# A recurrent step's input gate seeded into PSUM, and its two half sums added by one reduction

## What is computed

```
xw = einsum('ntd,dh->nth', x, Wx) + b
def step(h_prev, xw_t):
    h_next = tanh(xw_t + h_prev @ Wh)
    return h_next, h_next
x = x + scan(step, h0, xw)
```

## Time and profile before

| | |
|---|---|
| median of three runs | 1470.11 us |
| the profiled execution, its own time | 1471.73 us |
| its span | 1469.9 us |
| mean granted TensorE clock | 0.985 |
| TensorE busy | 1432.0 us (97%) |
| VectorE busy | 994.8 us (68%) |
| ScalarE busy | 659.7 us (45%) |
| first addition of step 0 starts | 32.02 us |
| products of the last step start | 1204.97 us |

### The profile page before, as it was taken

How to read it: one execution, slowest core, us unless ns; L and a number is a source line. 1 busy time by engine, 2 the same in 40 slices (tenths; PEclk the granted TensorE clock), 3 DMA queues, 4 the chain that set the end, 5 groups by cost and what they waited for, 6 DMA issues and landing times. The chain is left out here.

```text
span 1469.9 us, 49910 instructions
## 1 busy us (share of the span) xinstructions
PE 1432.0 (97%) x21212; PEld 1130.0 (77%) x21212; DVE 994.8 (68%) x2704; ACT 659.7 (45%) x2200; POOL 689.6 (47%) x555
## 2 busy tenths in 40 slices
PE   8889999999999999999999999999999998899998
PEld 6558888888888888888888888888887777577776
DVE  5334757575757575757575757575757679998894
ACT  4445454545454545454545454545444444233332
POOL 3432444444444444444444444444433446788774
PEclk8899999999999999999999999999999999999999
DMA  9750333333333323333323333333224547989994
GB/s 374 282 194 6 52 67 53 67 52 67 53 66 52 67 52 67 52 67 53 67 52 67 53 67 52 67 53 66 45 45 87 142 104 124 277 316 334 342 328 147
DMA packets 442337, 168.16 MB, mean 114 GB/s; under 512 B 406481, under 2 KB 409681, under 8 KB 438914
## 3 DMA queue, kind: packets, MB, share of 16 engines
q1 hardware_dynamic: 441584, 164.53, 44.4%
q10 hardware_dynamic: 530, 0.44, 0.1%
HBM read 96.78 MB, written 68.16 MB: 112 GB/s over the span
## 5 line engine op out<-in xcount | busy, mean ns | idle before, releaser
L462 PEld LDWEIGHTS recb<-hs,scanS 128*128 128x128 f16 x16384 | 443.7, 96 | 170.9 <-DVE hs L1265 169.6
L462 PE MATMUL recb<-hs,scanS 128*128 128x32 f16 x16384 | 495.0, 177 | 18.0 <-DVE hs L1265 17.9
L697 ACT ACTIVATE hs<-pre 128x64 f16<-128x64 f32 x512 | 131.7, 257 | 623.1 <-DVE pre L1257 622.3
L1255 DVE TENSOR_TENSOR pre<-recb,xw 128x64 f32<-128x64 f32 x512 | 115.1, 225 | 265.3 <-PE recb L462 261.4
L1120 DVE RECIPROCAL gates<-gates 128x64 f32<-128x64 f32 (+1 forms) x484 | 258.4, 555 | 0.4
L1265 DVE TENSOR_TENSOR hs<-konst,hs 128x64 f16<-128x64 f32 x512 | 115.1, 225 | 136.6 <-ACT konst L698 136.6
L949 POOL TENSOR_TENSOR xt<-xt,hbuf 128x512 f32<-128x512 f32 (+1 forms) x65 | 99.0, 1523 | 175.4 <-ACT hbuf L701 175.4
L937 POOL TENSOR_TENSOR x1lo<-xt,x1hi 128x512 fp32r<-128x512 f32 x64 | 82.1, 1284 | 186.8 <-ACT x1hi L707 186.8
L955 POOL TENSOR_TENSOR gates<-gates 128x512 f32<-128x512 f32 x62 | 80.0, 1290 | 166.6 <-DVE gates L1120 166.6
L962 POOL TENSOR_TENSOR xt<-xt,pout 128x512 f32<-128x512 f32 x64 | 75.8, 1185 | 153.6 <-DVE pout L1146 153.6
L1257 DVE TENSOR_TENSOR pre<-recb,pre 128x64 f32<-128x64 f32 x512 | 114.9, 224 | 17.6
(11 more groups left out here) (221 smaller groups left out, 2760.5 us busy)
## 6 DMA issues: line engine op xcount, KB each, us to landing
xt<-in_x SPq DMA_DIRECT2D x64, 256.0 KB, 3.6
g_d<-gst SPq DMA_DIRECT2D x64, 256.0 KB, 3.9
n_d<-nst SPq DMA_DIRECT2D x64, 256.0 KB, 3.1
x_d<-xt SPq DMA_DIRECT2D x64, 256.0 KB, 3.1
out<-gates SPq DMA_DIRECT2D x63, 256.0 KB, 6.6
xt<-x_d SPq DMA_DIRECT2D x28, 512.0 KB, 5.1
stage<-in_w SPq DMA_DIRECT2D x11, 1024.0 KB, 7.3
xt<-g_d SPq DMA_DIRECT2D x14, 512.0 KB, 7.4
```

What stands on the lines that cost most here:

```text
L462: last = nc.tensor.matmul(rec[:, m].rearrange("p a b -> p (a b)"), w[:, k, m * P:(m + 1) * P], hs[:, k].rearrange("p a b -> p (a b)"), sta ...
L697: nc.scalar.activation(hs[:, :, 0, :], pre[t % 2][:], ACT.Tanh, scale=unscale).then_inc(s_h, 1)
L1255: nc.vector.tensor_tensor(pre0[:], rec[:, :, 0, :], xw[j % 2][:, t], ALU.add).then_inc(s_pre0, 1)
```

## The change

The bank `recb` is split into two halves of 128 columns, one for even and one for odd steps (`sums`). Behind the operation that reads one half, VectorE writes the seed of the next step into the other half: the x gate in the columns of the high part and zero in those of the low part, made by one multiplication of the gate with the two numbers 1 and 0 (`halves`, in PSUM). The products of a step then all accumulate. One reduction over both parts gives `pre`. Since only TensorE's own writes mark PSUM elements as ones to accumulate onto, one extra product over the 256 columns stands ahead of the loop; and the first step's products wait for the first seed.

```diff
@@ tiles
-        pre0, pre = sb("pre0", [P, C, B]), [sb(f"pre{e + 1}", [P, C, B]) for e in range(2)]
+        pre = [sb(f"pre{e + 1}", [P, C, B]) for e in range(2)]
...
-        rec = recb[:, 0:C * 2 * B].rearrange("p (c a b) -> p c a b", c=C, a=2)
+        sums = [recb[:, e * SUMS:(e + 1) * SUMS].rearrange("p (c a b) -> p c a b", c=C, a=2) for e in range(2)]
+        halves = recb[:, 2 * P:2 * P + 2]
@@ SyncE, before the early loads of the last block
-                    sp.wait_ge(s_pre0, TS * (NBLK - 1))
+                    sp.wait_ge(s_pre, TS * (NBLK - 1))
@@ TensorE, step
-                            last = nc.tensor.matmul(rec[:, m].rearrange("p a b -> p (a b)"), w[:, k, m * P:(m + 1) * P],
-                                                    hs[:, k].rearrange("p a b -> p (a b)"),
-                                                    start=(k == 0 and m == 0 and w is wh_hi), stop=(k == C - 1),
-                                                    skip_group_check=True)
+                            last = nc.tensor.matmul(sums[t % 2][:, m].rearrange("p a b -> p (a b)"), w[:, k, m * P:(m + 1) * P],
+                                                    hs[:, k].rearrange("p a b -> p (a b)"), start=False, stop=(k == C - 1), skip_group_check=True)
@@ TensorE, before the loop
+            pe.wait_ge(s_turned, 3)
+            nc.tensor.matmul(recb[:, 0:2 * SUMS], split["x"][0][:, 0, 0:P], x1hi[:, 0, 0:2 * SUMS], start=True, stop=True).then_inc(s_bits, 1)
             pe.wait_ge(s_sg, 3)
             pe.wait_ge(s_wh, 9)
-            pe.wait_ge(s_turned, 3)
+            pe.wait_ge(s_seed, 1)
@@ VectorE
+            def seed(j, t):
+                j, t = j + t // TS, t % TS
+                if j == NBLK:
+                    return
+                if t == 0 and j:
+                    dve.wait_ge(s_xw, C * (j + 1))
+                gate = xw[j % 2][:, t].unsqueeze(2).to_broadcast([P, C, 2, B])
+                keep = halves.unsqueeze(1).unsqueeze(3).to_broadcast([P, C, 2, B])
+                nc.vector.tensor_tensor(sums[t % 2], gate, keep, ALU.mult).then_inc(s_seed, 1)
...
-            dve.wait_ge(s_h0, 1)
+            dve.wait_ge(s_bits, 1)
+            nc.vector.memset(halves[:, 0:1], 1.0)
+            nc.vector.memset(halves[:, 1:2], 0.0).then_inc(s_h0, 1)
+            dve.wait_ge(s_h0, 2)
+            seed(0, 0)
             for j in range(NBLK):
                 for t in range(TS):
-                    if t == 0:
-                        dve.wait_ge(s_xw, C * (j + 1))
                     dve.wait_ge(s_rec, TS * j + t + 1)
-                    nc.vector.tensor_tensor(pre0[:], rec[:, :, 0, :], xw[j % 2][:, t], ALU.add).then_inc(s_pre0, 1)
-                    dve.wait_ge(s_pre0, TS * j + t + 1)
-                    nc.vector.tensor_tensor(pre[t % 2][:], rec[:, :, 1, :], pre0[:], ALU.add).then_inc(s_pre, 1)
+                    nc.vector.tensor_reduce(pre[t % 2][:], sums[t % 2].rearrange("p c a b -> p c b a"), axis=AX.X, op=ALU.add).then_inc(s_pre, 1)
+                    seed(j, t + 1)
```

More of the change, by code:

```diff
@@ L84 @@
 SLOTS = B * C
+SUMS = C * 2 * B
 def build(nc, a, out):
@@ L194, in build @@
                                     "s_hyp s_lr s_h0").split())
-        (s_x1, s_x1h, s_x1l, s_xp, s_xw, s_rec, s_pre0, s_pre, s_h, s_hb, s_hs, s_x2, s_x2h, s_x2l, s_lowd, s_f, s_i, s_c, s_fs, s_is, s_gs, s_r, s_fr,
+        (s_x1, s_x1h, s_x1l, s_xp, s_xw, s_rec, s_bits, s_seed, s_pre, s_h, s_hb, s_hs, s_x2, s_x2h, s_x2l, s_lowd, s_f, s_i, s_c, s_fs, s_is, s_gs, s_r, s_fr,
          s_in, s_g, s_n, s_zero, s_car, s_P, s_X) = (
-            sem("r_" + s) for s in ("s_x1 s_x1h s_x1l s_xp s_xw s_rec s_pre0 s_pre s_h s_hb s_hs s_x2 s_x2h s_x2l s_lowd s_f s_i s_c s_fs s_is s_gs s_r s_fr "
+            sem("r_" + s) for s in ("s_x1 s_x1h s_x1l s_xp s_xw s_rec s_bits s_seed s_pre s_h s_hb s_hs s_x2 s_x2h s_x2l s_lowd s_f s_i s_c s_fs s_is s_gs s_r s_fr "
                                     "s_in s_g s_n s_zero s_car s_P s_X").split())
```

## The result

Over 20 runs of each kernel the median goes from 1470.67 us (1464.08 to 1473.86) to 1466.57 us (1460.15 to 1469.88). The ratio is 0.9971, 95% interval 0.996 to 0.9982 (it is taken over all runs and so is not the quotient of the two medians): 4.3 us faster, between 2.6 and 5.9. The forecast was 1466.3, with a gain of 3.8. The profiled execution of the changed kernel, however, spans 1460.4 us, 9.5 less than the one before: over twice the measured gain.

What follows compares the result with a forecast made beforehand. TensorE's own queue bounds most steps; only steps where the VectorE and ScalarE chain ends last gain. Terms 0 - 2.6 - 1.2 = -3.8 us against the profiled 1471.73 give 1467.9, median forecast 1466.3 us, range 1459 to 1472.

Steps and rivals of the forecast that it cites:

- The middle blocks give nothing: Blocks 1 to 14: TensorE's queue ends last and the chain arrives 0.09 us early, so shortening it gains nothing.
- Rival A: Blocks 1 to 15: weight load starts beside the last large product, up to 0.02 us a step, 1460.4 us; chance 0.30.
- Each bound step gains the chain's 0.20: Steps where the chain ends last: 0.48 us of additions become a 0.28 reduction, 0.20 shorter, at least 0.10.
- B: Rival: the reduction reads PSUM slowly, 0.38 us, half the gain, -1.4 us or 1468.7; chance 0.14.
- Start and step 12 cancel: Block 0: start 1.4 us later, 8 bound steps before step 12 give 1.6 back; net 0, between -0.2 and +0.7.
- Behind step 12 and in block 15: Block 0's 13 bound steps after step 12 gain 2.6 us; block 15 and the end gain 1.2 together.
- the last chain: End of block 15: the last chain gives 0.20 us, and the tail moves with the last state.
- TensorE's own limit: Block 15, steps 28 to 30: five large products limit a step to 2.06 us; steps 29 and 30 gain 0.14 each.
- C: Rival, reciprocal steps: reduction and seed hold VectorE over 0.55 us, so it bounds, +18 us, about 1487; chance 0.13.
- I would be wrong if the step changed in blocks 2 to 14 at all: Sign in the changed profile: block starts stay 73.4 us apart in blocks 2 to 14.

Runs made afterwards that it cites:

- experiments 8 to 10: 8: kernel before, reduction first, gate added after, no seed, 1554.97 us; 9: same, reduction's result in PSUM, 1475.47; 10: changed kernel, numbers 1 and 0 in SBUF, 1494.38.

## Why the prediction was right

Its four terms hold, each counted from the start of the gate's addition or within its stage.

- *The middle blocks give nothing.* Shown: one more tanh there is free, a second is not, and the slack between is 0.27 us a step. Rival A is out as far as this margin reaches. The state was ready at +1.00, before the sixth large product started at +1.03, and the weight load still came at +1.26. The state led that product by only 0.03 us; an earlier one was not tried. The rule of the Trainium skill that I had weighed against it (TensorE: Matmul & The Clock Gate, "The mechanism", a weight load overlaps a product in flight only on other rows of the array) forecast that. It does not describe the loads between the large products, which start with a product on all 128 rows; the same section also lets a load go ahead into a background weight buffer, which I had left out, and no row tells which buffer a load takes. So it is the outcome that agrees and not the rule as a whole.
- *Each bound step gains the chain's 0.20.* 2.20 to 2.01. The reduction is 0.292 and not 0.279, so 0.19; B and its 0.38 are out.
- *Start and step 12 cancel.* The start costs 1.62 instead of 1.40, the steps before 12 give back 1.5, but the transfer came later with the start, so step 12's products are 0.72 later behind the gate's addition, first profile against first and second against second: the upper end of the term (-0.2 to +0.7), not its middle. With the transfer moved the wait is gone and block 1 starts 0.9 us earlier, so nothing else stood behind it.
- *Behind step 12 and in block 15.* From step 12's products to block 1 the second profile of the kernel before takes 45.2 us and the changed kernel 42.1, both at full clock: 3.1 instead of 2.6. The 13 steps give what I said; 0.3 more is the rest of step 12 and 0.2 step 18, which I had not counted. Block 15 up to its last step takes 71.6 in the first profile of before and 70.7 in the second of the changed kernel, both of which have the cadence of 2.280 in this block: 0.9, where my terms without the last chain were 1.0. (The other two profiles give 72.3 and 71.1; the four pairings lie between 0.5 and 1.6.) Steps 29 and 30 stop at 2.06, TensorE's own limit, as forecast.

Together +0.7 - 3.1 - 0.9 - 0.2 = -3.5, beside -3.3 to -3.7 from profiles of one cadence (-2.8 to -3.0 counted from the gate's addition), and -4.3 (-5.9 to -2.6) from all runs. The last chain's 0.2 stands in the sum as forecast: from the last step's first operation to the end the kernel before takes 264.0 twice and the changed one 264.5 and 264.0, so the profiles do not show it. That the median came within 0.3 us of the forecast is partly luck. Two errors of opposite sign, +0.7 at step 12 and -0.5 behind it, nearly cancel, and each median depends on how many of its runs fall into which heap.

C did not come: reduction and seed hold VectorE for 0.40 us, under the 0.55 from which it would have decided. It was nearer than I knew. I had priced the seed at 0.29 by a row with one input in SBUF and one in PSUM without saying that this mattered, and the run with the numbers in SBUF shows the kind of loss that C describes, VectorE held too long by the seed, at +28 us.

What I got wrong is a sentence on how to read the changed profile: "I would be wrong if the step changed in blocks 2 to 14 at all". It did change in the profile, by 0.0133 a step, without being the change's doing. The changed profile shows 9.5 us of gain, of which 5.5 are this cadence in blocks 2 to 14, and some 2 are steps around block 1's start that ran at a lower granted clock in the profile before: the first step of block 1 took 3.46 us there, 2.29 after, and 2.23 in the second profile of the kernel before. The 2 us that remain are fewer than the 3.5 of the terms, in part because this one profile has the slower cadence in block 15 and a tail that took 0.5 longer.

## What to carry to other kernels

A shorter chain pays only in the steps in which it ends last; count these in the timeline and price the rest at nothing, even when the wait just behind the chain names it as its releaser. Look at where both inputs of a VectorE operation lie before it goes into a chain: with both in SBUF it waited here for GpSimd's operation to end, and moving one of them, even a constant, to PSUM decided over 28 or 80 us. And profile the old kernel twice before explaining a difference between two single profiles.

## What the runs showed of the hardware

- Two inputs in SBUF against GpSimd: a 64-element addition takes 0.225 us with GpSimd idle and 0.54 in the mean with GpSimd at work; with one input in PSUM always 0.224. A delayed addition ended 0.08 to 0.09 us behind the end of GpSimd's operation in all 217 cases, a delayed seed 0.15 to 0.16 us behind it in all 218; an operation that met only the last 0.15 us was not delayed. The Trainium skill (SBUF — State Buffer, "Who interferes with whom") has the rule, that a VectorE instruction with two SBUF inputs contends with a GpSimd instruction that reads SBUF and one with a single SBUF input, outside the two-port modes, does not; experiments 8 to 10 agree with both halves of it.
- The same program runs its loop of 38 products at 2.280 or 2.293 us a step, with TensorE busy throughout and a granted clock of 1.00. Blocks 2 to 14 of a profile all have the same of the two, and block 15 can have the other (2.293 and then 2.280 in the first profile of the kernel before, the reverse in that of the changed kernel). In the slower one the steps are alike, in the faster one 2.263 and 2.297 alternate. What chooses between them stays open; no run here was made to tell.
- VectorE can set the starting value of a sum in PSUM that TensorE's products then add to, 128 columns in 0.285 us. Here one product of TensorE had written the columns before; no run leaves that out. Reading and writing one bank in one operation costs nothing: the seed took 0.290 with the numbers in SBUF and GpSimd idle.
